# Two interleave ratios in the program order of a transformer block: 4 to 3 in weight preparation, 6 to 3 in normalisation

## The reference, cut to what matters

```python
xn = layernorm(x)                                     # x: (16, 2048, 1024) f32
# attention, 16 heads of 64
q, k, v = xn @ wq.T, xn @ wk.T, xn @ wv.T
q_mag, k_mag = softplus(q), softplus(k)
q_embed = stack([q_mag*cos(f), q_mag*sin(f)])         # (.., 128) per head
k_embed = stack([k_mag*cos(f+bias), k_mag*sin(f+bias)])
attn = softmax(q_embed @ k_embed.T / 8) @ v
# feed-forward part
gf = sigmoid(gelu(gelu(mean_s(xn) @ g1 + ..) @ g2 + ..) @ g3 + ..)   # one number per sequence
out = xn
for _ in range(3):
    tf = sigmoid(gelu(gelu(gelu(out @ w1) @ w2) @ w3) @ w4)
    out = out + (0.1 + ar * (0.7*gf + 0.3*tf - 0.5) * 2) * twist(out)
return x + attn @ wo.T + out
```

## Time and profile before

| | before |
|---|---|
| time, median of 2 runs | 4094.39 us (4058.82 to 4129.96) |
| the profiled execution | 4064.61 us, span of its slowest core 4063.1 us |
| spans of its eight cores | 4038.4 to 4063.1 us |
| granted TensorE clock, mean | 0.800 to 0.805 of full speed |
| PE busy, share of the span | 65% |
| ACT busy | 40% |
| DVE busy | 35% |

### The profile page before, as it was taken

How to read it: one execution, slowest core, us unless ns; L and a number is a source line. 1 busy time by engine, 2 the same in 40 slices (tenths; PEclk the granted TensorE clock), 3 DMA queues, 4 the chain that set the end, 5 groups by cost and what they waited for, 6 DMA issues and landing times.

```text
span 4063.1 us, 35717 instructions; the slowest of 8 cores (4038.4 to 4063.1 us)
## 1 busy us (share of the span) xinstructions
PE 2654.8 (65%) x10486; PEld 1082.8 (27%) x10486; DVE 1402.5 (35%) x2359; ACT 1644.2 (40%) x2082; POOL 40.5 (1%) x80
## 2 busy tenths in 40 slices
PE   0446777677777966667424576677767787756664
PEld 0222322223222223323212222232223212323322
DVE  4354223332333323333345333312332242333333
ACT  2215666566654022222123465566656701222221
POOL 1000000000000000000000000000000000000000
PEclk9958988888987577778666788888889856877777
DMA  6540001100100222121133011001110003022121
GB/s 155 134 91 24 6 24 27 25 18 11 27 19 6 47 81 73 42 83 52 62 120 101 24 26 27 16 11 27 27 25 17 5 13 78 32 94 78 36 83 57
DMA packets 84371, 193.23 MB, mean 48 GB/s; under 512 B 25559, under 2 KB 28632, under 8 KB 84184
## 3 DMA queue, kind: packets, MB, share of 16 engines
q1 hardware_dynamic: 73240, 175.74, 14.3%
q0 software_dynamic: 10944, 15.21, 2.7%
HBM read 134.27 MB, written 41.94 MB: 43 GB/s over the span
## 4 chain that ended last, share of the span: by engine, by line
PE 47%; DVE 22%; DMA 12%; issue 11%; ACT 5%; SPq 1%; DVEq 1%; POOL 0%; ACTq 0%; POOLq 0%
PE ps_w L170 24%; PE ps_s L170 15%; PE ps_pv L170 8%; DVE stream L170 6%; DMA xt<-x 4%; ACT pt L170 3%; DMA xt<-ffn_s 3%; DMA tmp<-qmag 3%; DVE vp L170 2%; DVE qh L170 2%; DVE ke L170 1%; SPq L170 1%; DMA ke<-kmag 1%; DMA w1t<-cnw 1%; DVE tmp L170 1%
## 5 line engine op out<-in xcount | busy, mean ns | idle before, releaser
L170 ACT ACTIVATE pt<-ps_s,cpool 128x1024 bf16<-128x1024 f32 x1024 | 1085.5, 1113 | 786.8 <-PE ps_s L170 783.6
L170 PE MATMUL ps_pv<-pt,vp 128*65 128x512 bf16 x2048 | 667.2, 410 | 287.7 <-DVE tmpB L170 228.0
L170 PE MATMUL ps_s<-qh,ke 128*128 128x512 bf16 x2048 | 668.3, 410 | 113.4 <-ACT pt L170 80.0
L170 PEld LDWEIGHTS ps_pv<-pt,vp 128*65 128x65 bf16 x2048 | 237.1, 118 | 573.5 <-issue 384.7
L170 PEld LDWEIGHTS ps_s<-qh,ke 128*128 128x128 bf16 x2048 | 174.5, 103 | 485.2 <-issue 409.1
L170 ACT ACTIVATE h<-ps_w,b1f 128x512 bf16<-128x512 f32 x192 | 132.0, 687 | 349.8 <-PE ps_w L170 349.8
L170 PE MATMUL ps_w<-ofm,w1t 128*128 128x512 bf16 x1024 | 252.4, 409 | 10.7 <-ACT ofm L170 10.7
L170 ACT CAST ofm<-ps_w 128x128 bf16<-128x128 f32 x256 | 49.6, 279 | 461.7 <-PE ps_w L170 461.6
L170 PE MATMUL ps_w<-ident,sbf 128*128 128x128 bf16 x512 | 64.7, 306 | 250.0 <-DVE sbf L170 250.0
L170 DVE COPY rowstg<-ps_pv 1x1024 f32<-1x1024 f32 x32 | 39.1, 1222 | 440.0 <-PE ps_pv L170 439.8
L170 DVE CAST vp<-ps_w 128x64 bf16<-128x64 f32 x512 | 115.7, 226 | 183.7 <-PE ps_w L170 155.8
(11 more groups left out here) (128 smaller groups left out, 2599.5 us busy)
## 6 DMA issues: line engine op xcount, KB each, us to landing
xt<-x SPq DMA_DIRECT2D x128, 512.0 KB, 4.0
ffn_s<-xt SPq DMA_DIRECT2D x32, 512.0 KB, 2.6
xt<-ffn_s SPq DMA_DIRECT2D x32, 512.0 KB, 4.1
out<-stream SPq DMA_DIRECT2D x32, 512.0 KB, 3.0
ke<-kmag SPq DMA_DIRECT2D x32, 256.0 KB, 2.9
qh<-qmag SPq DMA_DIRECT2D x32, 256.0 KB, 3.4
tmp<-qmag SPq DMA_DIRECT2D x32, 256.0 KB, 3.8
wqt<-wqT_s SPq DMA_DIRECT2D x16, 256.0 KB, 2.8
```

The source lines that it names most:

```text
L170: inst = getattr(engine, op.method)(*op.args, **op.kwargs)
```

## The change

Both edits change one number: how many steps of the first generator are emitted per step of the second. No instruction is added or taken away.

```diff
@@ -686,7 +686,7 @@
                         if not ln_done:
                             ln_done = next(gl, _SENT) is _SENT
                     next(gp, None)
-                drive((gp, 4), (gen_projembed(0, midyield=False), 1))
+                drive((gp, 3), (gen_projembed(0, midyield=False), 1))
             else:
                 for _ in gen_prep(False):
                     pass
@@ -856,7 +856,7 @@
               reads=["smallt"], writes=["smallt3"])
             yield
 
-        drive((gen_norm(), 6), (gen_gc(), 1))
+        drive((gen_norm(), 3), (gen_gc(), 1))
 
         if s == 0:
             for c in range(CK):
```

## The result

| | before | after |
|---|---|---|
| time, median of all runs | 4077.13 us (14 runs) | 4101.21 us (15 runs) |
| ratio of the runs | 1 | 1.0082, 95% interval 1.0056 to 1.0109 |
| the profiled execution | 4064.61 us | 4101.56 us |
| spans of its cores | 4038.4 to 4063.1 us | 4080.5 to 4100.0 us |

A forecast was written before the change was run, and what follows sets the result against it. PE, busy 65% of the span, was taken to set the end most of the time, so stage borders decide. 4064.6 + 14 (edit 1) + 9 (edit 2) = 4087.6, said as 4088 us; range 4062 to 4132.

The forecast's parts named there:

- The loss in the start stage: Weight preparation up to attention's start: the wqt load is issued at 300.4 instead of 286.61, +13.8 us, taken as +14.
- The gain of v: Preparation: v's last transposes end at 239.6 instead of 253.1, by five fewer tiles (9 us) and shorter store waits (4.5 us).
- the chain behind v: From v's memset to the q group of pair 1: both heads' products and copies among wo tiles, 27.3 us more.
- Edit 2's cost: Normalisation: four more gcv insertions +7.2, wait behind n26 +4.3, tiny matmuls behind n29 -1.2; n31 ends 10.3 us later per sequence.
- behind n26: Normalisation: PE must wait for n26's product on DVE, the copy and hand-offs, then run the small matmuls, +4.3 us.
- The rival of lost overlap: Normalisation: each of four insertions inside a pair also takes the next pair's overlap, 10.8 us more, 4098; chance 0.13.
- What edit 2 gets back: Wait for w1t behind the normalisation: shorter by 7.9 us in sequence 0 and 3.7 in sequence 1.
- SP's traffic leaves the window: Wait for w1t: SP's loads are issued some 7 us before n31 is done, returning 7.9 and 3.7 us.
- edit 1 hidden: Preparation: attention's start does not move, since the last tiles' stores run beside head 1; only edit 2 remains, 4074; chance 0.20.
- larger way back: Behind the normalisation: edit 2 costs only 5.5 us and edit 1 nothing, 4070, or 4051 without the net's tail; chance 0.12.
- late global weights: Normalisation: `xt<-gcw` loads exceed their 4.9 us lead, PE stands at each of 16 insertions, 4146 and above; chance 0.03.
- The limit of 2%: Whole kernel: a measurement can tell about 2%, 81 us; faster 0.01, within it 0.94, slower 0.05.

## Why the prediction was right or wrong

**The mechanisms held.** Both edits lengthen waits and nothing else. Edit 1 brings the v part forward and the attention start back; edit 2 pushes w1t by its insertions. Every row the prediction named moved its way: k group before 176 (172.97), v's last transposes near 240 (DVE's last cast of them at 240.61), no wo store before 250 (256.82), 118 to 120 us of normalisation (118.1), woTtp ahead of w1t. Some came later than named: the first scores at 298.10 for 293, the wqt load at 307.24 for 300, the q group of pair 1 at 310.51 for 304, and waits of 28.8 and 26.2 us for 26 and 23.

**The loss in the start stage was mis-sized: +13.8 forecast, +18.8 measured.** The gain of v was right: 13.5 forecast, 13.0 measured by the medians (v's memset 101.0 us after the first q group before, 88.0 after). The term that failed is the chain behind v, 31.8 us more from v's memset to the q group of pair 1 where 27.3 were forecast. Its copies between partitions were priced from the earlier trace rows at 3.0 us, and 4.4 us for the pair. After, as medians over eight cores from issue to use, they took 5.5 and 5.8 us for head 0 (in core 1 245.61 to 250.90, 255.30 to 261.13) and 3.6 and 4.8 us for head 1. These excesses are 2.5, 1.4, 0.6 and 0.4 us, together 4.9 of the 5.0 missing. Why the same copies are slower was not tested by itself. They now stand behind casting loads and stores of 256 KB instead of the small wo stores, and in the run at 4 to 1 with one store of 256 KB per wo tile the first copy took 4.3 us instead of 3.0, which points to the large stores. SP's eight issues per tile, which the forecast counted on the path, proved to be 5 of the added 19 us.

**Edit 2's cost was right, +10.3 per sequence forecast, +9.3 and +10.5 measured.** The terms held as a sum: an insertion took 1.80 us (1324.55 to 1326.35), and behind n26 core 1 lost some 4 us. The rival of lost overlap fell: behind a `gcv` matmul inside a pair the next two steps run side by side (1326.35 and 1326.57). The drain at a change of tiling mode that the Trainium skill names ("TensorEngine Tiling (Array Packing)", section Key Properties) did not prevent this. The next `rcpsB` step then waits 1.75 us for its row, so that the insertion is still paid in full.

**What edit 2 gets back was mis-sized by two and a half: 11.6 forecast, 4.6 measured** (5 to 7 by the wider comparison above). The step that failed is "SP's traffic leaves the window": 7.9 us of its engine time in sequence 0 and 3.7 in sequence 1 should have gone. It lost 1.9 us in each (11.9 to 10.0, 6.7 to 4.8). Three things were wrong in that step.
- The windows of the earlier trace rows reach past the end of the wait, and so count traffic that came too late to delay w1t: 4.46 MB for core 5's first window, of which 3.78 MB lie between 1403.74 and 1437.48, and 2.88 MB for the second, of which 2.36 MB lie between 3379.91 and 3406.96.
- What stands behind on SP moves up. In sequence 1 a `gcw` load and two x loads were to leave, and did, but the fifth x load came in: 2.35 MB fell to 1.57, not by 1.3 MB. In sequence 0 I had left the two early x loads as pure gain, while they are still on their way when w1t starts: they are issued from 1430.53 on, behind `woTtp`, and the first w1t load at 1434.20. 3.21 MB stayed in the wait, where the forecast left about 2.
- The price of 1.5 us for an x load held where it could be tested (two loads fewer, 3.6 and 2.9 us less). For `woTtp` 7.7 us was too much: the wait of sequence 0 fell by 3.1 us without it at 6 to 1, and by 1.3 at 3 to 1.

**The sum.** 5.0 us from the copies and 7.0 from the return, less 0.8 in the normalisations, are the 11.2 us between 22.8 and 34.0. The rivals "edit 1 hidden" and "larger way back" erred the same way, but further. The late global weights never appeared. Both large errors made the forecast too low, so almost nothing cancelled, and the time lies inside the range because the range was wide. The upper end of the range was added wrongly: 4117 and half of the 71 us between the two runs shown is 4153, not 4132.

**The verdict it was put in.** The limit of 2% that I took was too coarse: with this many runs the interval reaches only 0.27% to either side. A surplus of 23 us over the profiled execution should have been called a small, measurable loss.

## What to carry to other kernels

When two instruction streams are interleaved by a ratio, count what is left of the longer one when the shorter ends: side work that is pushed behind the main chain stops being free, and the price jumps when whole pieces are left (131, 136, 156 us for ratios 5, 4 and 3). When an insertion sits in a loop that gates the next stage's loads, each one moves those loads, and hiding its tail behind a wait that moves with it gains nothing. Price a copy or a DMA by the rows of the traffic it will meet. And before subtracting a transfer from a window, ask what stands behind it in its queue and will take its place, and end the window where the wait ends.

## What was not expected of the hardware

- SP's traffic in the loaded part of the wait cost its own engine time: with two x loads of 0.5 MB fewer, 3.5 us of 16 engines, the wait was 3.6 and 2.9 us shorter. In the first 5 us, where the casting loads filled the engines only by half, 1.5 MB of SP's cost little. With one x load beside them, w1t and w2t (3.15 MB written) took 21 to 22 us of all engines and kept PE waiting for 24.0 and 25.0 us.
- Eight stores of 32 KB held SP for 3.6 us where one of 256 KB with the same runs of 256 B was issued in 0.36 us, with the stage 7.5 to 12.5 us shorter.
- A copy of 256 KB between partitions took 3.0 us before and 5.5 us in the changed order, from issue to use, as medians over eight cores.
